# A block kernel with attention over channels and four experts: the last 48 rows of v get their 3x3 convolution on VectorE, expert weight pieces are split in twelve steps

## The reference, cut to what matters

```python
# block 1: attention over channels
xn = layernorm over channels (x)                      # twice: plain, then with ln_w, ln_b
qkv = einsum('bchw,oc->bohw', xn, w_qkv)              # 576 channels
qkv = depthwise 3x3 convolution of qkv with w_dw      # zero padding at the border
q, k, v = split(qkv); each times spatial_interaction
q, k = q / ||q||, k / ||k||                           # norm over all positions
attn = softmax(q k^T * temperature)                   # per head, 24 x 24
x = x + w_proj @ (attn v)
# block 2: mixture of experts on the 16384 tokens t (192 numbers each)
probs = softmax(layernorm(t) @ gate_w + gate_b)       # 4 experts, the best 2 are used
h = gelu(layernorm(t) @ w1[e] + b1[e])                # 192 -> 768
y = h @ w2[e] + b2[e]                                 # 768 -> 192
t = t + sum over the 2 chosen experts of weight * y
```

## Time and profile before

| | |
|---|---|
| runs | 1996.16, 1995.72, 1994.73 us; median 1995.72 |
| profiled execution, first to last instruction | 1993.4 us, of which no time around the span is given; the median of the runs is 2.3 us above it |
| busy: TensorE, VectorE, ScalarE, GpSimd | 1838.7, 1379.8, 1277.2, 1123.5 us |
| phase 1 | 0 to 619 us |
| 16 units ahead of the beats | 630 to 674 us |
| beats 0 to 11 | 674 to 835 us |
| blocks 0 to 3 (beats 12 to 15) | 835 to about 905 us |
| further blocks | 905 to 1905 us |
| output | 1905 to 1993 us |

### The profile page before, as it was taken

One profiled execution on the slowest core, in us unless ns is written; L12 is line 12 of the kernel. 1 busy time (PEld: TensorE's weight loads), 2 busy tenths in 40 slices (PEclk: granted clock), 3 DMA queues, 4 the chain that ended last, 5 costly groups with the idle time before them and its releaser, 6 DMA issues.

```text
span 1993.4 us, 36026 instructions
## 1 busy us (share of the span) xinstructions
PE 1838.7 (92%) x9782; PEld 1502.9 (75%) x9782; DVE 1379.8 (69%) x3382; ACT 1277.2 (64%) x2468; POOL 1123.5 (56%) x1079
## 2 busy tenths in 40 slices
PE   5799999999795989898999999999999999999956
PEld 3566666666564767688989989899898888888844
DVE  3789999999777474667676686776766655555532
ACT  3688888888674435465666666666667667676622
POOL 3666666666663015476767676767677676344320
PEclk9899999999896999899999999999999999999977
DMA  3453323333333798777788878788787877656569
GB/s 97 147 148 93 92 89 93 92 91 92 99 111 95 228 290 275 263 221 216 211 229 215 227 213 228 213 229 224 216 226 195 242 204 202 171 155 180 129 184 338
DMA packets 254367, 361.97 MB, mean 182 GB/s; under 512 B 27396, under 2 KB 183940, under 8 KB 254212
## 3 DMA queue, kind: packets, MB, share of 16 engines
q1 hardware_dynamic: 191556, 278.59, 46.3%
q0 software_dynamic: 50880, 60.59, 15.0%
q10 hardware_dynamic: 11776, 20.98, 3.0%
HBM read 222.76 MB, written 137.30 MB: 181 GB/s over the span
## 4 chain that ended last, share of the span: by engine, by line
PE 57%; DMA 4%; DVE 3%; POOL 2%; issue 2%; ACT 1%; SPq 1%; POOLq 0%; DVEq 0%; ACTq 0%
PE bank L1804 21%; PE bank L1820 14%; PE bank L1787 7%; PE bank L1821 6%; PE bank L1847 4%; DMA xn<-acc_scratch 3%; PE bank L1839 3%; POOL xs_scratch L1251 1%; POOL acc_scratch L1266 1%; PE bank L1869 1%; DMA acc_scratch<-yo,tix 1%; DMA xs<-xs_scratch 0%; PE bank L1872 0%; DVE hl L1758 0%; ACT L1319 0%
## 5 line engine op out<-in xcount | busy, mean ns | idle before, releaser
L1266 POOL DMA_INDIRECT acc_scratch<-yo,tix x268 | 439.0, 1638 | 304.2 <-DVE yo L1647 238.0
L1804 PE MATMUL bank<-x_all,w1b 128*128 128x512 f32 x2010 | 548.8, 402 | 1.0 <-ACT hf L1319 1.0
L1820 PE MATMUL bank<-w_hl,hh 128*128 x1608 | 495.5, 360 | 6.7 <-DVE hl L1758 5.8
L1319 ACT ACTIVATE hf<-bank,b_col 128x512 f32<-128x512 f32 x402 | 276.7, 688 | 335.5 <-PE bank L1804 335.4
L1758 DVE TENSOR_TENSOR hl<-hf,hh 128x512 fp32r<-128x512 f32 x402 | 277.2, 690 | 272.5 <-ACT hh L1322 272.3
L1821 PE MATMUL bank<-w_hl,hl 128*128 x1608 | 404.9, 252 | 0.0
L1804 PEld LDWEIGHTS bank<-x_all,w1b 128*128 128x128 f32 x2010 | 348.2, 188 | 55.1 <-ACT hf L1319 1.4
L625 DVE SCALAR_TENSOR_TENSOR bank<-zwin,wdw,bank 128x512 f32<-128x512 f32 (+2 forms) x462 | 336.3, 734 | 43.4 <-PE bank L731 34.8
L1820 PEld LDWEIGHTS bank<-w_hl,hh 128*128 128x128 f32 x1608 | 302.1, 188 | 40.9 <-issue 10.4
L1821 PEld LDWEIGHTS bank<-w_hl,hl 128*128 128x128 f32 x1608 | 306.1, 190 | 17.4
L1251 POOL DMA_INDIRECT xs_scratch<-xn,idx x256 | 262.2, 1024 | 85.1 <-issue 75.7
(11 more groups left out here) (261 smaller groups left out, 2902.3 us busy)
## 6 DMA issues: line engine op xcount, KB each, us to landing
w1b<-w1s_scratch SPq DMA_DIRECT2D x134, 768.0 KB, 5.1
xs<-xs_scratch SPq DMA_DIRECT2D x67, 522.0 KB, 6.0
xtok_scratch<-xtok SPq DMA_DIRECT2D x32, 384.0 KB, 2.7
v_scratch<-zv SPq DMA_DIRECT2D x64, 192.0 KB
vc_scratch<-yo ACTq DMA_DIRECT2D x64, 192.0 KB, 4.5
vd<-vc_scratch SPq DMA_DIRECT2D x64, 192.0 KB
xtok<-xtok_scratch SPq DMA_DIRECT2D x32, 384.0 KB, 7.3
acc_scratch<-x SPq DMA_DIRECT2D x32, 384.0 KB, 5.5
```

The costliest lines, as they stand in the source:

```text
L1266: nc.gpsimd.indirect_dma_start(acc_dram, bass.IndirectOffsetOnAxis(ap=tix[:, J % 4, t:t + 1], axis=0), yo[:, J % YN, t, :], None, compute_ ...
L1319: nc.scalar.activation(hf[:, k % 3, :], lb[k % 2][:, :], ACT.Gelu, bias=b1_col[:, bass.ds(exp_of[J] * CH + k, 1)]).then_inc(gelu, 1)
L1804: last = nc.tensor.matmul(lb[k % 2][:, :], w[:, q, :], v[:, J % 2, :], start=(i == 0), stop=(i == 4))
L1820: nc.tensor.matmul(yb[t][:, 0:2 * C], hh[:, k % 3, cols], w, start=(k == 0), stop=False, skip_group_check=True)
```

## The change

- NV, the number of bands that TensorE convolves, goes from 16 to 10 (rows 0 to 79). There are 48 units; those with u from 32 on have 2 bands (256 columns) in place of 4. The list of units by beat is 2, 2, 2, 2, 3, 3, 2, 4, 4, 4, 4.
- The rows 80 to 127 of v are stored as they are into `vn_scratch`. They are convolved in 9 **own units** d of 128 partitions (64 channels x 2 bands of 8 rows, or 32 x 4): ScalarE does the middle tap (`own_head`, 128 x 1024 elements), VectorE the other eight (`own_tap`, 128 x 1024 each), at k = 2, 4 and 5 of the beats 12 to 35, three in a beat, 72 in all. SyncE loads and stores the own units. Projections of steps 20 to 23 wait for own units 0 to 2, those from 24 on for all.
- One input buffer of the own units lies over tensors of phase 1 (`keep`). To have room for the other and for the outputs, `xn` has XN = BATCH + 2 = 6 slots in place of 8, and the gate's compare buffers and `tri` are smaller.
- The 24 pieces are done two in a step, in steps 1 to 4, 6 to 9, 19, 20, 28 and 29, all low parts on GpSimd. Phase 1 has two loops (steps 11 to 18 and 21 to 26) in place of one (5 to 26); the other steps are written out.
- From step 16 on a projection step is 4 rows that follow each other.

```diff
-            PIECES_AT = {1: (0, 4), 2: (4, 8), NB - 5: (8, 12), NB - 4: (12, 16), NB - 2: (16, 20), NB: (20, 24)}
-            LOAD_AT = {0: 0, 3: 1, NB - 3: 2, NB - 1: 3}
+            PIECE_STEPS = (1, 2, 3, 4, 6, 7, 8, 9, NQ - 1, NQ, NB - 4, NB - 3)
+            PIECES_AT = {i: (2 * k, 2 * k + 2) for k, i in enumerate(PIECE_STEPS)}
+            LOAD_AT = {0: 0, 5: 1, 10: 2, NB - 5: 3}
...
-                    if i.static and i.val == NB:
-                        for p, g in pieces_of(i):
-                            dve.wait_ge(e_hi, p + 1)
-                            dve.wait_ge(e_lo, p)
-                            hi, lo, raw = pieces[p]
-                            nc.vector.tensor_tensor(lo, raw, hi.bitcast(FP32), ALU.subtract).then_inc(e_lo, 1)
...
-        UNITS = 4 * BANDS
+        UNITS = 3 * BANDS
...
-        for n, m in enumerate([2, 2, 2, 2, 3, 3, 3, 8, 8, 8, 7]):
+        for n, m in enumerate([2, 2, 2, 2, 3, 3, 2, 4, 4, 4, 4]):
...
+        slots_d = [(n, k) for n in range(n_a, n_beats) for k in (2, 4, 5)][:UD * len(TAPS_D)]
+        tap_at = {slot: divmod(i, len(TAPS_D)) for i, slot in enumerate(slots_d)}
+        head_at = {(n, k - 1): d for (n, k), (d, i) in tap_at.items() if i == 0}
...
-            XN = 2 * BATCH
+            XN = BATCH + 2
...
+                def own_head(d):
+
+                    if d == 0:
+                        act.wait_ge(ld_wt, 96)
+                        act.wait_ge(cv_t, UNITS)
+                    act.wait_ge(ld_n[d % 2], stored_d(d + 1, d % 2))
+                    if d >= 2:
+                        act.wait_ge(st_n[d % 2], stored_d(d, d % 2))
+                    nc.scalar.activation(n_out[:, d % 2, :, :], n_in[d % 2][:, 1:RV + 1, :], ACT.Identity, scale=wtap[:, d, 4:5]).then_inc(hd_ok, 1)
...
+                def own_tap(d, i):
+
+                    ky, kx = divmod(TAPS_D[i], KX)
+                    to, of = slice(max(0, 1 - kx), min(W, W + 1 - kx)), slice(max(0, kx - 1), min(W, W - 1 + kx))
+                    if i == 0:
+                        dve.wait_ge(hd_ok, d + 1)
+                    else:
+                        dve.wait_ge(nt_ok, 8 * d + i)
+                    nc.vector.scalar_tensor_tensor(out=n_out[:, d % 2, :, to], in0=n_in[d % 2][:, ky:ky + RV, of], scalar=wtap[:, d, TAPS_D[i]:TAPS_D[i] + 1],
+                                                   in1=n_out[:, d % 2, :, to], op0=ALU.mult, op1=ALU.add).then_inc(nt_ok, 1)
...
+                        if (n, k) in tap_at:
+                            own_tap(*tap_at[n, k])
```

More of the change, by code:

```diff
@@ L104, in wait, with steps @@
     eng.wait_ge(sem, value)
-def steps(eng, emit, first, last, lo, hi, setup=None):
-    assert (hi - lo) % 2 == 1
-    for n in range(first, lo):
-        emit(Step(0, n))
-        if setup and n == first:
-            setup()
-    with eng.Fori(0, (hi - lo + 1) // 2) as j:
-        for u in (0, 1):
-            emit(Step(j, lo + u))
-    for n in range(hi + 1, last + 1):
-        emit(Step(0, n))
+def steps(eng, emit, first, last, loops, setup=None):
+    n = first
+    for lo, hi in (*loops, (last + 1, last)):
+        for n in range(n, lo):
+            emit(Step(0, n))
+            if setup and n == first:
+                setup()
+        if lo < hi:
+            assert (hi - lo) % 2 == 1
+            with eng.Fori(0, (hi - lo + 1) // 2) as j:
+                for u in (0, 1):
+                    emit(Step(j, lo + u))
+        n = hi + 1
 def build(nc, x, spat, ln_w, ln_b, w_qkv, w_dw, w_proj, temperature, gate_w, gate_b, w1, b1, w2, b2, out):
@@ L237, in build, with below @@
             row_z = sem("row_z")
-            FIRST, LAST, LO, HI = -2, NB + 2, 5, NB - 6
+            FIRST, LAST = -2, NB + 2
+            LOOPS = ((11, NQ - 2), (NQ + 1, NB - 6))
+            def below(i):
+                return (i.val if i.static else i.c) < NQ
             def slots(n):
@@ L371, in step @@
                         load_experts(LOAD_AT[i.val])
-                steps(sp, step, FIRST, LAST, LO, HI)
+                steps(sp, step, FIRST, LAST, LOOPS)
                 sp.wait_ge(ld_zero, 32)
@@ L454, in step @@
                         pool.wait_ge(r_ok, 2 * b.val + 2)
-                    for n, g in pieces_of(i) if not (i.static and i.val == NB) else []:
+                    for n, g in pieces_of(i):
                         pool.wait_ge(e_hi, n + 1)
@@ L600, in setup @@
                     act.wait_ge(ld_w, 16 * N_LD_W)
-                steps(act, step, FIRST, LAST, LO, HI, setup)
+                steps(act, step, FIRST, LAST, LOOPS, setup)
             @blk.vector
@@ L855, in setup @@
                     pe.wait_ge(gq_lo, 2)
-                steps(pe, step, FIRST, LAST, LO, HI, setup)
+                steps(pe, step, FIRST, LAST, LOOPS, setup)
         NG = NB // BATCH
@@ L906, in row @@
         def row(s, t):
+            if s >= SPREAD:
+                return ROWS * s + t
             return Q_STEPS * (ROWS * (s // Q_STEPS) + t) + s % Q_STEPS
         def rows_of(s, first=0, count=ROWS):
-            return slice(row(s, first), row(s, first + count - 1) + 1, Q_STEPS)
-        assert Q_STEPS == RV
+            return slice(row(s, first), row(s, first + count - 1) + 1, 1 if s >= SPREAD else Q_STEPS)
         def unit(u):
@@ L977, in build @@
             zl_c = sb(p2, "zl_c", [128, 4, W + 2], F32R)
+            wtap = sb(p2, "wtap", [128, UD, 9])
+            n_in = [sb(p2, "n_in", [128, (RV + 2) * W]), keep]
+            n_in = [t[:, :].rearrange("p (r w) -> p r w", w=W) for t in n_in]
+            n_out = sb(p2, "n_out", [128, 2, RV, W])
             hf = sb(p2, "hf", [128, 3, TOK])
```

193 lines of the change are left out of this document (140 added, 53 removed).

## The result

| | before | after |
|---|---|---|
| median of the runs, us | 1995.85 (4 runs, 1994.73 to 1996.16) | 1965.74 (4 runs, 1964.06 to 1969.05) |
| profiled execution, us | 1993.4 | 1965.6 |
| busy: TensorE, VectorE, ScalarE, GpSimd, us | 1838.7, 1379.8, 1277.2, 1123.5 | 1796.5, 1430.3, 1257.6, 1142.4 |

The ratio is 0.9856, 95% interval 0.9838 to 0.9875.

The account below looks back on a forecast made before the run. TensorE was taken as the bound in the blocks, serial scatter laps in the beats after the change. Terms -20.7 - 6.2 + 5 + 1 + 10.8 = -10.1 us gave 1985.6 us as median; eight-in-ten range 1970 to 2002.

Parts of the forecast that it names:

- Beats 0 to 11: Convolution units from beat 0 until `normalise(9)`: fewer and halved units, but scatter waits in series; 6.2 us gained.
- four laps in series: From step 6's moments to `normalise(9)`: moments, `inverse_std`, scatter, landing, `normalise`, one after another; 17.1 us each, 67.5 in all.
- The landing: Beats 7 to 11, time from issue of a scatter's last transfer until it has landed: 3.0 us, other end 6.0.
- The fourth rival: Beats 7 to 11: six slots do not bind, GpSimd scatters ahead of the moments; some 22 us more gained, 1963; chance 0.06.
- Phase 1: Projection steps at the start: spreading the pieces ends buffer waits, and VectorE's last subtractions go; 20.7 us gained, 16 to 23.
- Copies lie one to one on the path: Phase 1: ScalarE's copies of pieces lengthen a step by their full time, 11 us in all after the change.
- Blocks 0 to 3: `normalise(10)` to `(12)` wait for scatters of steps 4 to 6: 5 us lost, 3 to 8; taps add 1.
- group 2's tail in beat 15: The only cost put on taps in beats 12 to 15: 1 us lost.
- Gate beats: Groups 3 and 4 (beats 21 to 23, 29 to 31): VectorE lacks room for taps; 5.4 us a group, 10.8 lost.
- ordinary beats: Beats without gate or placing: three taps (3.75 us) just fit VectorE's 3.6 us idle; 0 lost, other end 0.6 a beat.
- The second rival: Taps not hidden in ordinary beats either: sixteen beats at 0.6 to 0.75 us, 10 to 12 us lost, 1997; chance 0.20.
- The first rival: `normalise(6)` to `(12)`: landings stay at 6 us, six serial laps 3 us longer each, 18 us, 2003.6; chance 0.15.

Follow-up runs that it names:

- s_order: Changed kernel with GpSimd doing `inverse_std` first, then the 8 transfers of one step, in beats 8 to 10; 1989.86 us against 1965.74.
- t12: Changed kernel with only the first twelve taps (beats 12 to 15) cut to 8 elements; 1958.53 us against 1965.74.
- f_first: Changed kernel with the scatter of step 0 ahead of `inverse_std` in beat 7; 1955.11 us against 1965.74.
- m4: Changed kernel with unit 0's taps in beats 8 to 11, then four a beat in 16 to 21, 24 to 29, 32 to 35; 1958.43 us.
- fm4: Changed kernel with the edits of m4 and f_first together; 1946.79 us against 1965.74.
- m4b: Changed kernel with four taps a beat in beats 12, 13, 16 to 21, 24 to 29 and 32 to 35; 1951.25 us against 1965.74.
- fm4b: Changed kernel with the edits of m4b and f_first together; 1937.92 us, ratio to the kernel before 0.9711.

## Why the prediction was wrong, step by step

1. **Beats 0 to 11, -6 forecast, -28.5 measured: the step that failed.** The prediction said "GpSimd starts a step's scatter only after that beat's `inverse_std`" and priced four laps in series, "4 x 13.87". The timeline before has a transfer at 772.56, right behind those of step 0. Steps 0 and 1 go in one piece, those of steps 2 and 3 ahead of that beat's `inverse_std`, and 1.6 us to the first transfer, 32 transfers at 1.27 us and three `inverse_std` of 1.5, 47 us together, fill nearly all of the 48.7 between the moments of step 6 and `normalise(9)`, with six slots or eight. With the order as it was read, s_order lost 25.5 us here, and the miss is 22.3: its stage is 3.0 us shorter than in the kernel before, where the prediction had 6.2. Its first half was right: between `normalise(0)` and the moments of step 6 the kernel gained 13.5 us (forecast 13.0).
2. **The landing, 3.0 forecast.** From the last transfer's issue to the `normalise` that waited it was 6.6 (727.94 to 734.55), 3.0 (to 741.10), 7.5 (to 757.37) and, for `normalise(10)`, 5.9 us: three of four at the other end of the earlier trace rows. The DMA share there is 0.81 where it was 0.92, and the median of all 32 landings 5.1 us where it was 6.0, not 3.0. The mistake ran against the first and hid in it: with the order as it was read, the laps of s_order are 18 to 19 us, not 17.1.
3. **The fourth rival was nearest.** "The six slots do not bind", chance 0.06, 1963 us. Its mechanism was half right: the scatters of steps 1 to 3 do go ahead of that beat's `inverse_std`, that of step 0 does not. The slots do bind, twice for long, but what they cost in these beats is 0.6 us. It was given 0.06 on the same misread order as in point 1. That its 1963 is so near to the measured 1965.7 is luck in part: 6 us more in phase 1 stand against 10 lost in blocks 0 to 3 and the gate beats, and the 36 us that it starts from are worked out nowhere.
4. **Phase 1, -20.7 forecast, -26.9 measured.** "Copies lie one to one on the path" was wrong. This is the second step that failed. The slack of 0.7 us a step was in the trace (0.53 and 0.69 us ahead of two operations at 496 to 498 us) but in no step that had copies, and only those were read. Of 11 us for the copies some 2 remained: the 29 steps from the start of step 2 last 488.2 us where 29 x 16.77 is 486.3. That is most of what the first part was short by (23.9 us gained at the first operation of the last step, 15.5 forecast). The last step gave 3.0 us (23.9 to 26.9 at `rinv`), where 5 were forecast for its subtractions; no run takes these apart from its copies, which went too.
5. **Blocks 0 to 3, +6 forecast, +13.5 measured.** The slots' part was right (5 forecast, 5.5 and 6.7 in two pairs of kernels). The taps' part was not: 1 us for "group 2's tail in beat 15", where beats 14 and 15 carry gate and placing as 22 and 23 do, 6.0 us by t12.
6. **Gate beats, +10.8 forecast, +13.2 measured; ordinary beats, 0 and 0.** The length of a tap (1.25, measured 1.27) and the mechanism were right. Group 4 cost 5.0 us, where 5.4 were forecast, group 3 8.3; in f_first group 3 cost 5.1 too, and in the 3.2 between the granted clock fell in the one kernel and not in the other (below).
7. The second rival (taps show in ordinary beats) is refuted with room to spare: the 13 such beats of the changed kernel kept their length, and of 64 with four taps from beat 16 on (16 in each of m4, fm4, m4b, fm4b) 60 were longer by 0.15 us at most. The other four are 0.2 to 3.9 us longer; in the two longest TensorE waits 1.9 and 2.1 us for the load of `xs`, a DMA, and not for VectorE. But the reason that the rival gave, that VectorE or GpSimd stretch each other, is real on GpSimd's side: transfers of 0.96 us took up to 2.01, and an `inverse_std` operation of 0.20 took 1.14. The Trainium skill ("SBUF — State Buffer", "SBUF: two separate sides") lets a VectorE operation with two inputs in SBUF and a GpSimd one that reads SBUF shut each other out for a whole operation. The `inverse_std` in m4 agrees, since it ends with the tap. The prediction left out the condition that GpSimd reads SBUF, and put the rule down to the fourth rival where it belongs to this one. The first rival's landings came for the most part, without its laps.
